# A two-part graph network on one core: layer 3's state by way of device memory, and the vector engine's sums and edges placed anew

## The reference

```python
# part 1
adj_norm = adj / (sum(adj, axis=-1) + 1e-8)
h = relu(concat([x, adj_norm @ x]) @ W0 + bias)
x = layernorm(x + h)
# part 2: A = (adj != 0), h = x
for l in range(5):
    m   = h @ weight[l]
    agg = einsum('bij,bid->bjd', A, m)
    gi, gh = agg @ w_ih.T + b_ih, h @ w_hh.T + b_hh
    r, z = sigmoid(i_r + h_r), sigmoid(i_z + h_z)
    n = tanh(i_n + r * h_n)
    h = (1 - z) * n + z * h
out = layernorm(x + h * mask)
```

## Time and profile before

| | before |
|---|---|
| median of 3 runs | 609.21 us (609.12 to 609.42) |
| the profiled execution's own time | 608.95 us |
| its span, first to last instruction | 606.9 us |
| granted TensorE clock, mean | 0.992 of full speed |
| PE busy | 589.7 us, 97% |
| DVE busy | 513.5 us, 85% |
| ACT busy, POOL busy | 419.4 us each, 69% |
| DMA | 73.55 MB |

### The profile page before, as it was taken

The page is one execution under the profiler, slowest core; times in us unless marked ns, Lnnn a source line. Parts: engine busy times, 40 slices in busy tenths (PEclk is TensorE's granted clock), DMA queues, the critical chain, the costliest instruction groups (busy, mean ns, idle before and its releaser), DMA issues.

```text
span 606.9 us, 9921 instructions
## 1 busy us (share of the span) xinstructions
PE 589.7 (97%) x2733; PEld 479.4 (79%) x2733; DVE 513.5 (85%) x1151; ACT 419.4 (69%) x777; POOL 419.4 (69%) x335
## 2 busy tenths in 40 slices
PE   7999999999999999999999999999999999999992
PEld 6678788888888888888888888888888888877771
DVE  5986969898998989899898989989898898966677
ACT  5767685958778595876868587685867768555451
POOL 0645464878868687886869688687977868755343
PEclk9999999999999999999999999999999999999996
DMA  8713122454344446334444534445453433010101
GB/s 271 294 35 114 54 76 88 134 180 121 123 151 112 161 127 190 121 121 146 115 154 138 190 112 130 141 115 158 138 174 110 148 138 95 10 53 10 44 0 53
DMA packets 74002, 73.55 MB, mean 121 GB/s; under 512 B 5760, under 2 KB 49280, under 8 KB 73984
## 3 DMA queue, kind: packets, MB, share of 16 engines
q1 hardware_dynamic: 73712, 73.20, 37.7%
q10 hardware_dynamic: 272, 0.13, 0.1%
HBM read 56.00 MB, written 17.30 MB: 121 GB/s over the span
## 4 chain that ended last, share of the span: by engine, by line
PE 91%; DVE 4%; DMA 1%; issue 1%; ACT 1%; SPq 1%; POOL 0%; POOLq 0%; DVEq 0%
PE ps_tok L1405 12%; PE ps_tok L1412 12%; PE ps_r L1269 6%; PE ps_r L1270 6%; PE ps_r L1271 6%; PE ps_z L1269 6%; PE ps_z L1271 6%; PE ps_z L1270 6%; PE ps_b L1271 3%; PE ps_b L1269 3%; PE ps_b L1270 3%; PE ps_in L1270 3%; PE ps_in L1271 3%; PE ps_hn L1271 3%; PE ps_in L1269 3%; PE ps_hn L1270 3%
## 5 line engine op out<-in xcount | busy, mean ns | idle before, releaser
L686 POOL TENSOR_TENSOR z_h<-z_gate,h 128x512 f32<-128x512 f32 x80 | 110.2, 1377 | 24.1 <-ACT z_gate L893 24.0
L676 POOL TENSOR_TENSOR h_lo<-h,h_hi 128x512 fp32r<-128x512 f32 x64 | 88.5, 1383 | 53.8 <-ACT h_hi L708 53.8
L811 ACT ACTIVATE ps_in<-ps_in,gru_bias 128x512 f32<-128x512 f32 x80 | 52.8, 660 | 53.6 <-DVE ps_in L1132 53.5
L1405 PE MATMUL ps_tok<-edges,tok_hi 128*128 (+1 forms) x320 | 87.8, 396 | 0.7 <-ACT tok_hi L708 0.7
L1412 PE MATMUL ps_tok<-edges,tok_lo 128*128 (+1 forms) x320 | 87.6, 396 | 0.0
L1248 DVE SCALAR_TENSOR_TENSOR r_hn<-ps_hn,gru_bias,r_gate 128x512 f32<-128x512 f32 x80 | 59.6, 745 | 28.1 <-ACT r_gate L883 26.9
L615 POOL TENSOR_TENSOR adjt_lo<-adjt_in,adjt_hi 128x512 fp32r<-128x512 f32 x56 | 72.1, 1312 | 4.3 <-ACT adjt_hi L708 4.3
L1405 PEld LDWEIGHTS ps_tok<-edges,tok_hi 128*128 128x128 f32 x320 | 59.7, 188 | 15.6 <-ACT tok_hi L708 0.9
L1412 PEld LDWEIGHTS ps_tok<-edges,tok_lo 128*128 128x128 f32 x320 | 59.9, 188 | 14.7 <-DVE tok_lo L919 0.3
L883 ACT ACTIVATE r_gate<-ps_r,rz_bias 128x512 f32<-128x512 f32 x80 | 55.2, 691 | 20.0 <-PE ps_r L1271 17.0
L1173 DVE SCALAR_TENSOR_TENSOR ps_in<-z_gate,ps_in 128x512 f32<-128x512 f32 x80 | 55.1, 689 | 10.9 <-ACT ps_in L811 8.6
(11 more groups left out here) (156 smaller groups left out, 1599.0 us busy)
## 6 DMA issues: line engine op xcount, KB each, us to landing
adjt_in<-in_adj_t_dram SPq DMA_DIRECT2D x14, 1024.0 KB, 5.4
adj_in<-in_adj_dram SPq DMA_DIRECT2D x14, 1024.0 KB, 5.3
rows<-passage SPq DMA_DIRECT2D x144, 64.0 KB, 2.0
passage<-early_blocks SPq DMA_DIRECT2D x24, 256.0 KB, 2.1
x_in<-in_x_dram SPq DMA_DIRECT2D x16, 256.0 KB, 3.8
xt_in<-in_x_t_dram SPq DMA_DIRECT2D x15, 256.0 KB, 3.0
out_dram<-y_out SPq DMA_DIRECT2D x15, 256.0 KB, 2.3
passage<-last_blocks SPq DMA_DIRECT2D x14, 256.0 KB, 2.1
```

Of the source, the lines that this page charges most:

```text
L676: nc.gpsimd.tensor_tensor(h_lo[new][:], h[new][:], raw(h_hi[new][:]), ALU.subtract).then_inc(s_h_lo, 1)
L686: nc.gpsimd.tensor_tensor(z_h[:], z_gate[:], h[own][:], ALU.mult).then_inc(s_zh, 1)
L1405: nc.tensor.matmul(ps_tok[:], tok_hi[:, c * P:(c + 1) * P], edges_from(c, unit[0]), start=c == 0, stop=False)
```

## The change

- Slot 4 joins the moved slots: layer 3's state is block-transposed by DVE in slot 2, stored, loaded, and made into `tok_hi` by ACT and `tok_lo` by POOL in slot 3. PE's four transposes in slot 3 and DVE's `tok_lo` go. The blocks use the buffer of layer 1's state, so the transpose also waits until that one has been stored.
- `mean_parts` moves from slot 2 to slot 3; `residual` moves behind `agg_lo(3)`, and all four `bn_stats` behind `h`.
- The edges: rows 2 and 3 of four (one instruction of 128x1024) in slot 0 between `own` and `r_hn`, row 0 in slot 2, row 1 in slot 3 between the statistics and `moments1` (128x512 each).
- POOL makes `tok_lo` in front of the power `rstd`, no longer behind.
- SP: the two transfers of layer 3's state stand in front of the load of `adjt`; `x` is loaded ahead of `adj`, and `adj` now waits for the edges of slot 3.
- The buffer `sum_of` goes; ACT's row sums write their unused output to `r_gate` or `y_out`, with a wait of ACT for its own sums in slot 1.

```diff
-MOVED = {slot: UNITS[slot][1] for slot in (1, 2, 3)}
+MOVED = {slot: UNITS[slot][1] for slot in (1, 2, 3, 4)}
...
-        return slot in (0, 1) and self.trips()
+        return slot in (0, 1, 2) and self.trips()
...
-        blocks = {4: early_blocks, 1: early_blocks, 2: late_blocks}
+        blocks = {4: early_blocks, 1: early_blocks, 3: early_blocks, 2: late_blocks}
...
                     store_state(w, 1)
                     load_state(w, 1)
+                    store_state(w, 3)
+                    load_state(w, 3)
                 if w.loads():
                     sp.wait_ge(s_adjt_lo, w.prepared(C, C) if w.first > 0 else C)
                     load_adjt(b)
                 if w.loads():
+                    sp.wait_ge(s_pre1, w.prepared(1, 1))
+                    load_x(b)
                     sp.wait_ge(s_row_sum, w.prepared(C, C) if w.first > 0 else C)
                     sp.wait_ge(s_edges, w.prepared(C, C) if w.first > 0 else C)
                     load_adj(b)
-                    sp.wait_ge(s_pre1, w.prepared(1, 1))
-                    load_x(b)
...
-                    if w.prepares() and slot == 3 and not w.leads():
-                        rstd1_of_batch()
                     if w.finishes() and slot == 2 and (w.prepares() or w.idles()):
                         last_norm()
                     if w.next_moved(slot):
...
+                    if w.prepares() and slot == 3 and not w.leads():
+                        rstd1_of_batch()
...
+                        if slot == 1 and w.prepares() and w.first > 0:
+                            act.wait_ge(s_row_sum, w.prepared(C, C))
...
-                    if slot == 1:
-                        dve.wait_ge(s_state_passed[4], w.passed(16))
+                    if slot in (1, 2):
+                        dve.wait_ge(s_state_passed[4 if slot == 1 else 1], w.passed(16))
...
                         if slot == 2 and not w.ramps():
-                            if w.first >= 3:
-                                dve.wait_ge(s_agg, w.last_layers())
-                            edge_half(0)
+                            edges_of((0,))
...
                         if slot == 3 and not w.ramps():
-                            residual(w)
-                            stats1_of(w, (0, 1))
+                            mean_parts(w)
...
                     if w.prepares() and slot == 3 and not w.ramps():
-                        stats1_of(w, (2, 3))
-                        dve.wait_ge(s_stats1, w.prepared(C, C))
+                        residual(w)
...
+                    if w.prepares() and slot == 3 and not w.ramps():
+                        stats1_of(w, range(C))
+                        dve.wait_ge(s_stats1, w.prepared(C, C))
+                        edges_of((1,))
...
-                        if slot == 2 and not w.leads():
+                        if slot == 2 and w.first == 1:
                             mean_parts(w)
-                            if not w.ramps():
-                                edge_half(1)
...
                             xw_parts(0)
+                            if not w.ramps():
+                                dve.wait_ge(s_adj_in, w.prepared(16, 16))
+                                if w.first >= 3:
+                                    dve.wait_ge(s_agg, w.last_layers())
+                                edge_half(1)
```

More of the change, by code:

```diff
@@ L309, in program @@
         own = sb("own", [P, C, D])
-        sum_of = sb("sum_of", [P, N])
         mean_t = sb("mean_t", [P, N])
@@ L348, in program @@
         late_blocks = sb("late_blocks", [P, Q, C, SQ])
-        blocks = {4: early_blocks, 1: early_blocks, 2: late_blocks}
-        passages = {k: nc.dram_tensor(f"passage{k}", [P, N], F32, kind="Internal").ap() for k in (1, 2, 4)}
-        rows = {k: sb(f"rows{k}", [P, Q, C, SQ]) for k in (1, 2, 4)}
+        blocks = {4: early_blocks, 1: early_blocks, 3: early_blocks, 2: late_blocks}
+        passages = {k: nc.dram_tensor(f"passage{k}", [P, N], F32, kind="Internal").ap() for k in range(1, LAYERS)}
+        rows = {k: sb(f"rows{k}", [P, Q, C, SQ]) for k in range(1, LAYERS)}
         ps_tok = bank("ps_tok")
@@ L432, in program @@
         s_last = sem("s_last")
-        s_state_blocks = {k: sem(f"s_state_blocks{k}") for k in (1, 2, 4)}
-        s_state_passed = {k: sem(f"s_state_passed{k}") for k in (1, 2, 4)}
-        s_state_rows = {k: sem(f"s_state_rows{k}") for k in (1, 2, 4)}
+        s_state_blocks = {k: sem(f"s_state_blocks{k}") for k in range(1, LAYERS)}
+        s_state_passed = {k: sem(f"s_state_passed{k}") for k in range(1, LAYERS)}
+        s_state_rows = {k: sem(f"s_state_rows{k}") for k in range(1, LAYERS)}
         s_blocks = sem("s_blocks")
@@ L719, in row_sum_of @@
                     act.wait_ge(s_row_sum, earlier)
-                nc.scalar.activation(sum_of[:] if c != 1 or earlier is not None else r_gate[:], of[:, c, :], ACT.Copy,
+                scratch = y_out[:].rearrange("p c d -> p (c d)") if of is second_adj or earlier is None and c == 0 else r_gate[:]
+                nc.scalar.activation(scratch, of[:, c, :], ACT.Copy,
                                      accum_out=row_sum[:, c:c + 1]).then_inc(s_row_sum, 1)
```

## The result

The changed kernel took 616.59 us (median of 6 runs, 614.81 to 620.3) against 609.24 (608.54 to 609.61) for the kernel before, measured beside it: a ratio of 1.0126, 95% interval 1.0099 to 1.0153. It is **1.3% slower**, where I had forecast 607.4, or 0.3% faster. The profiled execution took 615.23 us, its span 613.1, so 6.2 us more than the 606.9 of before. The granted clock was 0.994 against 0.992 before, so it isn't the clock.

The account below looks back on a forecast made before the run. The prediction took PE's issue of matmuls to bound the kernel: 608.95 - 5.3 (transposes) + 3.0 (slot 4 stall) + 0.5 (window 2) = 607.15 for the profiled execution, the median 0.26 above it, so 607.4 us; range 603.8 to 616.

Parts of the forecast that it names:

- PE, what is removed: Slot 3: four transposes take 0.36 us and 0.08 behind them, so 0.44 less a window, 5.3 us in 12.
- DVE, the stall in slot 4: DVE's steps sum to 7.70, agg_lo(4) comes 0.40 later against 0.72 of room: PE stalls 0.25 a window, 3.0 us.
- rival B: Slot 3: DVE's edges wait for POOL's tok_lo, agg_lo(4) another 0.3 to 0.4 late; 611.0 us, chance 0.24.
- The term for the weights: Slot 4: a PE wait also shows the otherwise hidden load of the weights, 0 to 0.19 us, taken as 0.13.
- DVE, the rest: Slot 2 has less work, slot 0's added edges (0.76) fit 0.90 of idle time, slot 3's mean_parts replaces equal work.
- POOL. Nothing: Slot 3: tok_lo (1.30) ahead of the power doesn't hold it up; the power ends 209.3, x1 is next at 209.5.
- Window 2: New order with transposes and DVE's tok_lo kept: agg_lo(4) later by 0.40 and 0.64 against 0.72; 0.5 us, once.
- The state's way, transfers, SP's queue: Layer 3's state through device memory: tok_hi and tok_lo in time by 1.5 and 1.0 us, reordered loads cost nothing.
- A: Everything hides: DVE makes up the 0.25 in slot 4; 603.9 us, chance 0.14.
- D: PE's transposes cost nothing that counts, or are given back elsewhere; 609.2 us, chance 0.05.
- C: Slot 0's edges also wait for POOL, r_hn(0) is 0.7 late and delay spreads to agg_lo(2); 617 us, chance 0.22.
- My list of what would show it: Signs: windows 0.19 us shorter, 12 slot 4 waits of 0.1 to 0.3; wrong if these exceed 0.4 or rows land late.

Follow-up runs that it names:

- pe_only: The kernel before, with only one of PE's four transposes of slot 3 left in windows 3 to 14: 605.23 us, ratio 0.9928.
- half_slot2: The changed kernel with only the half of the edges in slot 0 moved back to slot 2: 612.64 us, ratio 1.0062 to the kernel before.
- half_slot0: The changed kernel with mean_parts, residual, two statistics and edge row 1 back in their old slots, half the edges still in slot 0: 606.76 us, ratio 0.9959.
- h0_first: The changed kernel with ACT and POOL making h0's parts ahead of h(4)'s in slot 4: 622.64 us, ratio 1.0238 to the kernel before.
- hi_early: The changed kernel with only ACT's h0_hi moved earlier, ahead of r_gate in slot 4: 622.16 us, ratio 1.0222 to the kernel before.
- edges_s2: The changed kernel with row 1 of the edges moved from slot 3 to slot 2, beside row 0: 609.32 us, ratio 1.0001 to the kernel before.
- low_waits: The changed kernel with POOL's tok_lo of slot 3 waiting for DVE's edges there: 622.59 us, ratio 1.0226 to the kernel before.

## Why the prediction was wrong, step by step

**PE, what is removed: right.** 0.44 forecast, 0.45 measured in slot 3, 0.33 for three of the four transposes in *pe_only*.

**DVE, the stall in slot 4: the right place, mis-sized.** Forecast 0.25, measured 0.40. The sum of the steps was 0.3 short in the window shown: 0.13 for the edges' wait for the statistics, which the rows of before don't have since other work stood between there, and 0.16 for the edges behind POOL. The second is rival B, a part of its 0.3 in the regular windows and 1.1 in window 3. The term for the weights erred the other way: I took 0.13, but in the rows above `agg_lo(4)` ends at 215.84 and `ps_r` starts at 215.90, while before `ps_r` started 0.75 behind the end of `agg_lo(4)`. So 0.69 of delay is free, not 0.72 - 0.13 = 0.59, and the weights cost 0.03. *half_slot2*, without rival B, shows 0.25 since its steps take 7.80 instead of 7.70 and its weights 0.03 instead of 0.13: two errors that cancel.

**The step that failed is "DVE, the rest", with "POOL. Nothing".** There I asked of slot 0 only if the edges fit, and of POOL only if its own new operation makes something late. I didn't follow `h(4)`, 0.40 later on DVE and 0.44 later against PE by my own terms, through ACT and POOL to its second consumer. All its rows were in the trace of before:

```profile
211.60 0.68 DVE L1074 TENSOR_TENSOR h<-z_h,ps_in 128x512 f32<-128x512 f32 x1
```

```profile
214.70 1.30 POOL L681 TENSOR_TENSOR h_lo<-h,h_hi 128x512 fp32r<-128x512 f32 x1 [0.38 <-ACT h_hi L708]
```

```profile
216.48 0.39 PE L1269 MATMUL ps_hn<-h_hi,whh_hi 128*128 128x512 f32 x1
```

`h(4)` starts 211.60 - 208.14 = 3.46 after the start of slot 4; `h0_lo` is done 1.38 after the start of slot 0 (214.62), and PE's `ps_hn` starts 1.86 after it. These rows alone leave 0.48 of room, and my 0.84 is more than that; by the runs the room is 0.3, half of what slot 4 has. It cost 11 x 0.34 = 3.7 us, the largest missing term.

**Window 2: mis-sized.** Forecast 0.5, measured 1.32. I had set the lateness against the room of `agg_lo(4)`; PE's wait is for DVE's `tok_lo` in slot 3, which comes behind four statistics and the edges and has less room.

**With the measured terms** the sum closes: 607.15, + 1.8 (slot 4 over the forecast's 6.73, summed over windows 4 to 14) + 1.1 (the same in window 3) + 3.7 (slot 0) + 0.8 (window 2) + 0.3 (slot 0 of the first window behind the repeated ones, 6.74 against 6.47 in *half_slot0*) + 0.56 (in front of window 2) = 615.4, and the profiled execution took 615.23.

**The state's way, transfers, SP's queue: right** to 0.1 us in regular windows. I had not foreseen window 3's loads of 2.61 us.

**The rivals.** A and D fell. B is real and the smaller part. C had the right sum, 617, by luck, and the wrong mechanism: the edges of slot 0 do wait for POOL (they take 0.81 to 1.31 us for 0.76) and make `r_hn(0)` late, but slot 1 absorbs it, and no wait in slot 2 appears. *half_slot0* keeps that delay and is faster than before. C's chance was for a spreading delay, and one spread, only from slot 4 and into slot 0.

**My list of what would show it** did its work: waits in slot 4 over 0.4 us, and waits at a place that I hadn't named.

## What to carry to other kernels

When an engine's results come later, list every consumer of each late result, also those two engines on, and read the room of each in the trace of before; the nearest consumer needn't be the one with the least room. A gain on the bounding engine is a loss of room for all the others, so subtract it everywhere before an order is packed tighter. And move as little as the change needs: here the new path for the state pays (-0.4%) once only the half of the edges leaves slot 2, and it was the rest of the reshuffle that lost 10 us.

## What the hardware showed that I had not expected

The wait between DVE and POOL strikes whatever instruction of its kind comes next, and its price is about the rest of the other's instruction, not the size of one's own: a 128x4 `var` took 1.07 us, a row of edges 1.56 for 0.43, `xt_lo` 1.83 for 0.79. POOL pays as well when DVE was first: 1.75 for 1.29 at `z_h`. DVE's instructions with a PSUM operand, the statistics and the aggregates kept their times beside a busy POOL in these traces (`r_hn` 0.74, `agg_lo` 0.68). So to start POOL earlier can cost more than it gives: *h0_first* and *hi_early* removed or shrank a wait of 0.34 and lost 6 us each.

What stays open: why the rows of layer 3's state land late in window 3, so that `tok_hi` starts 0.7 to 1.2 us later against PE than in most other windows, in every kernel that sends this state by device memory (SP's four loads take 2.6 to 2.9 us there in the changed kernel, *edges_s2*, *half_slot2* and *low_waits*, but 1.73 in the others), and why some runs have a microsecond more outside their span.
